# One added to keys and queries by a product of ones in PSUM, and elu+1 as the greater of z+1 and a clipped exponential

## The reference

```python
def _phi(x):
    return jax.nn.elu(x) + 1.0
...
x_norm = _rmsnorm(x, norm_weight)
k = _phi(jnp.einsum('btd,fd->btf', x_norm, Wk))
v = jnp.einsum('btd,ed->bte', x_norm, Wv)
...
def step(M, kv):
    k_t, v_t = kv
    v_pred = jnp.einsum('bf,bfd->bd', k_t, M)
    surprise = jnp.linalg.norm(v_t - v_pred, axis=-1, keepdims=True)
    delta = k_t[:, :, None] * v_t[:, None, :]
    M = M + eta_c[None, :, None] * surprise[:, :, None] * delta
    return (_ln2(M), None)
...
q = _phi(jnp.einsum('btd,fd->btf', x_norm, Wq))
mem_out = jnp.einsum('btf,bfd->btd', q, M)
```

## Time and profile before

| what | value |
|---|---|
| times of three runs | 258.69, 259.81 (median), 259.9 us |
| span of the profiled execution, first to last instruction | 258.2 us |
| what lies around that span, from the times shown | 0.5 to 1.7 us |
| PE busy | 245.4 us, 95% of the span |
| DVE, ACT, POOL busy | 206.3, 186.8, 112.7 us |
| share of PE in the chain that ended last | 66% |
| stretch in which keys and queries are formed | about 13 to 39 us |

### The profile page before, as it was taken

How to read it: one execution, slowest core, us unless ns; L and a number is a source line. 1 busy time by engine, 2 the same in 40 slices (tenths; PEclk the granted TensorE clock), 3 DMA queues, 4 the chain that set the end, 5 groups by cost and what they waited for, 6 DMA issues and landing times.

```text
span 258.2 us, 5143 instructions
## 1 busy us (share of the span) xinstructions
PE 245.4 (95%) x1665; PEld 160.8 (62%) x1665; DVE 206.3 (80%) x694; ACT 186.8 (72%) x459; POOL 112.7 (44%) x148
## 2 busy tenths in 40 slices
PE   7798799999999999999999999999999999999993
PEld 2257554567674458688777767976975444444482
DVE  5998789999968898998899896897623897666684
ACT  1588499986637797887757899989923997777730
POOL 9698300000001689988655795987880000000000
PEclk9999799999999999999999999999999999999999
DMA  7720000000004704000000000000000000000004
GB/s 198 198 57 3 0 1 3 1 0 3 1 1 175 316 3 164 3 0 1 4 0 3 0 0 0 5 0 3 0 0 3 0 0 0 3 3 0 0 30 139
DMA packets 8303, 8.50 MB, mean 33 GB/s; under 512 B 1745, under 2 KB 7378, under 8 KB 7762
## 3 DMA queue, kind: packets, MB, share of 16 engines
q1 hardware_dynamic: 7442, 7.65, 9.1%
q10 hardware_dynamic: 832, 0.49, 0.7%
HBM read 7.09 MB, written 1.05 MB: 32 GB/s over the span
## 4 chain that ended last, share of the span: by engine, by line
PE 66%; DVE 16%; POOL 8%; ACT 4%; issue 3%; DMA 2%; DVEq 0%; SPq 0%; POOLq 0%; ACTq 0%
PE PS L930 11%; PE PS L929 11%; PE PS L902 8%; PE PS L879 7%; PE PS L892 4%; POOL arena L1461 4%; POOL arena L1462 3%; PE PS L693 3%; PE PS L646 3%; PE PS L701 2%; DMA x<-L_attn_x 2%; DVE mxb L1981 2%; DVE arena L1967 2%; PE PS L530 2%; PE PS L685 1%
## 5 line engine op out<-in xcount | busy, mean ns | idle before, releaser
L929 PE MATMUL PS<-arena 128*128 128x512 f16 x128 | 48.5, 379 | 0.0
L930 PE MATMUL PS<-arena 128*128 128x512 f16 x128 | 48.5, 379 | 0.0
L2039 DVE TENSOR_TENSOR arena<-arena 128x512 f32<-128x512 f32 x32 | 22.2, 693 | 13.0 <-ACT arena L1385 13.0
L879 PE MATMUL PS<-arena 128*128 128x512 f32 (+3 forms) x80 | 31.9, 530 | 0.3 <-ACT arena L1354 0.3
L1384 ACT ACTIVATE arena<-PS,arena 128x512 f32<-128x512 f32 x32 | 22.9, 716 | 9.1 <-PE PS L930 9.1
L1461 POOL TENSOR_TENSOR arena<-arena 128x256 f32<-128x256 f32 x32 | 21.6, 674 | 15.4 <-DVE arena L1973 12.9
L1354 ACT ACTIVATE arena<-PS,lnt 128x512 f32<-128x512 f32 (+3 forms) x40 | 24.8, 628 | 2.9 <-DVE lnt L1988 2.8
L1462 POOL TENSOR_TENSOR arena<-arena,small 128x256 f16<-128x256 f32 (+1 forms) x36 | 23.8, 662 | 2.8
L1469 POOL CAST arena<-arena 128x512 f16<-128x512 f32 x2 | 1.3, 636 | 54.3 <-ACT x L1247 54.3
L1385 ACT ACTIVATE arena<-PS,arena 128x512 f16<-128x512 f32 x32 | 22.8, 713 | 0.0
L1981 DVE TENSOR_REDUCE mxb<-PS 128x1 f32<-128x512 f32 (+3 forms) x40 | 22.1, 601 | 0.0
(11 more groups left out here) (291 smaller groups left out, 615.5 us busy)
## 6 DMA issues: line engine op xcount, KB each, us to landing
arena<-h_T SPq DMA_DIRECT2D x2, 1024.0 KB, 6.3
x<-L_attn_x SPq DMA_DIRECT2D x4, 256.0 KB, 4.7
arena<-cos SPq DMA_DIRECT2D x1, 1024.0 KB, 4.8
arena<-sin SPq DMA_DIRECT2D x1, 1024.0 KB, 7.8
arena<-w_T SPq DMA_DIRECT2D x3, 256.0 KB, 3.3
out<-arena SPq DMA_DIRECT2D x2, 256.0 KB, 2.2
con<-shape_constants ACTq DMA_DIRECT2D x1, 192.5 KB, 3.5
out<-arena SPq DMA_DIRECT2D x1, 192.0 KB, 2.0
```

The costliest lines, as they stand in the source:

```text
L879: i = mm(PS[:, k, 0:cnt * P], qT1[:, t * P:(t + 1) * P], kT1[:, c * P:(c + cnt) * P], start=True, stop=not last)
L929: mm(bank(b), wH[:, k, m * P:(m + 1) * P], sH[:, k, cols], start=(k == 0), stop=False)
L930: i = mm(bank(b), wL[:, k, m * P:(m + 1) * P], sL[:, k, cols], start=False, stop=(k == HT4 - 1))
L2039: v.tensor_tensor(RP[m], FP[m], high, ALU.subtract).then_inc(rest_ready, 1)
```

## The change

A third kind of product enters PSUM behind each key and each query product. `one_more` multiplies one row of ones (64 columns as weights) with one row of 512 ones and accumulates it onto the 64 partitions that were just written, so that PSUM holds z+1. ACT then forms exp((z+1) - 1), with the -1 as a bias read from a new constant tile `minus_one`, straight from PSUM, and DVE takes max(min(exp, 1), z+1). The two instructions for a group of keys on ACT become one, and the three for a group of queries become two. The constant is one more memset on POOL; `SET` goes from 16 to 17, and `STATICS` from 8 to 4, since four of ACT's instructions that counted are gone. The copy of z+1 for the second group of queries stays where its max(z, 0) was, behind the four rows.

```diff
             def keys(g):
...
-                    i = mm(PS[F * h:F * h + F, 4 + g, :], wkT[:, :], xrT[:, ch * BANK:(ch + 1) * BANK], start=True, stop=True)
+                    mm(PS[F * h:F * h + F, 4 + g, :], wkT[:, :], xrT[:, ch * BANK:(ch + 1) * BANK], start=True, stop=False)
+                    i = one_more(PS[F * h:F * h + F, 4 + g, :])
                 i.then_inc(k_done, 1)
...
+            def one_more(z):
+
+                return mm(z, warm[0:1, 0:F], warm[0:1, :], start=False, stop=True)
...
-                    i = mm(PS[64 * hf:64 * hf + F, 4 + b, :], wqT[:, :], xrT[:, ch * BANK:(ch + 1) * BANK], start=True, stop=True)
+                    mm(PS[64 * hf:64 * hf + F, 4 + b, :], wqT[:, :], xrT[:, ch * BANK:(ch + 1) * BANK], start=True, stop=False)
+                    i = one_more(PS[64 * hf:64 * hf + F, 4 + b, :])
                 i.then_inc(q_done, 1)
...
-                o.need(o.did(f(e, bank(4 + g), ACT.Relu, scale=-1.0)))
-                f(e, e, ACT.Exp, scale=-1.0).then_inc(kphi_act, 1)
+                f(e, bank(4 + g), ACT.Exp, bias=minus_one).then_inc(kphi_act, 1)
...
+            def queries(b, linear):
+
+                act.wait_ge(q_done, b + 1)
                 cols = slice(b * BANK, (b + 1) * BANK)
-                if negative:
-                    return o.did(f(QE[:, cols], bank(4 + b), ACT.Relu, scale=-1.0))
-                f(QT[:, cols], bank(4 + b), ACT.Relu).then_inc(qphi_act, 1)
+                if linear:
+                    f(QT[:, cols], bank(4 + b), ACT.Copy).then_inc(qphi_act, 1)
+                else:
+                    f(QE[:, cols], bank(4 + b), ACT.Exp, bias=minus_one).then_inc(qphi_act, 1)
...
+            queries(0, False)
+            queries(1, False)
+            queries(0, True)
             table(0)
...
-            relus(1, False)
+            queries(1, True)
...
+            nc.gpsimd.memset(minus_one, -1.0).then_inc(set_once, 1)
...
-                v.scalar_tensor_tensor(out=KU[:, g, 0, 0:BANK], in0=bank(4 + g), scalar=0.0, in1=KE[:, c0 * HALF:c1 * HALF],
-                                       op0=ALU.max, op1=ALU.add).then_inc(k_ready, 1)
+                v.scalar_tensor_tensor(out=KU[:, g, 0, 0:BANK], in0=KE[:, c0 * HALF:c1 * HALF], scalar=1.0, in1=bank(4 + g),
+                                       op0=ALU.min, op1=ALU.max).then_inc(k_ready, 1)
...
-                    v.tensor_tensor(QT[:, part], QT[:, part], QE[:, part], ALU.add).then_inc(q_ready, 1)
+                    v.scalar_tensor_tensor(out=QT[:, part], in0=QE[:, part], scalar=1.0, in1=QT[:, part], op0=ALU.min, op1=ALU.max).then_inc(q_ready, 1)
```

More of the change, by code:

```diff
@@ L56 @@
 EO_EARLY = {9: (0, 1)}
-SET = 16
+SET = 17
 HIGH_TILES = 8
@@ L268, in program @@
         low_scale = small[:, 36:37]
-        eps2 = small[:, 37:38]
+        eps2, minus_one = small[:, 37:38], small[:, 15:16]
         mxs, nbs, rsum, rinv = (lnt[:, i, :] for i in range(2, 6))
@@ L476, in own_squares @@
             return CC[:, 2, 1:HALF + 1, :].rearrange("p j t -> p (j t)")[:, 0:(n - 1) * (L + 1) + 1:L + 1]
-        STATICS = 8
+        STATICS = 4
         def general_path(engine, run):
@@ L1106, in _ @@
                 f(CC[:, 2, r0:r0 + cnt, :], have[:, :, 2 * WINDOW:2 * WINDOW + L], ACT.Copy).then_inc(lanes_act, 1)
-            def relus(b, negative):
+            def queries(b, linear):
+                act.wait_ge(q_done, b + 1)
                 cols = slice(b * BANK, (b + 1) * BANK)
-                if negative:
-                    return o.did(f(QE[:, cols], bank(4 + b), ACT.Relu, scale=-1.0))
-                f(QT[:, cols], bank(4 + b), ACT.Relu).then_inc(qphi_act, 1)
+                if linear:
+                    f(QT[:, cols], bank(4 + b), ACT.Copy).then_inc(qphi_act, 1)
+                else:
+                    f(QE[:, cols], bank(4 + b), ACT.Exp, bias=minus_one).then_inc(qphi_act, 1)
             def table(k):
```

## The result

The changed kernel takes 266.28 us (median of 6 runs, 263.87 to 267.45), the kernel before 259.86 (6 runs, 258.69 to 261.38). The kernel is slower, and its median lies 0.5 us above the forecast. The profiled run took 265.5 us.

What follows compares the result with a forecast made beforehand. TensorE was taken to bound the kernel, with 66% of the chain. 1.25 + 1.75 - 0.55 + 3.65 - 0.15 = 5.95 us more gave 265.8 us, 2.3% slower, range 262.4 to 267.8.

Steps and rivals of the forecast that it cites:

- the pair is split: Keys and queries on PE: lower and upper half, side by side before, start about 1.4 us apart, ones between them.
- Halves together: Rival on PE: upper half overtakes the waiting ones; a group costs 0.37 us more, 260.4 us in all; chance 0.11.
- In order but no drain: Rival on PE: lower half's ones run beside the upper half; a group costs 1.08 us more, 262.7 us; chance 0.13.
- Ones free: Rival: ones cost nothing on PE and the pair stays whole; 0.7 us gained, 259.1 us; chance 0.03.
- What was put at nothing: POOL's memset of -1 (0.1 us without idle cover), DVE's sixteen query sums and L1586, and the counts: no cost.
- A change of footprint: PE, between a half and a product of ones: each change costs 0.15 us, bounds 0.10 and 0.30.
- a group: Each group of keys or queries on PE: 2.66 us instead of 0.91, so 1.75 us more.
- Keys, g = 0: First keys on PE: 1.75 us more, transposes behind swallow 0.5, so PE goes on 1.25 us late.
- Keys, g = 1: Second keys: products end 3.0 us late, one ACT pass fewer saves 0.55, DVE's sum is 2.45 late.
- Queries: Queries on PE start 2.45 us late and cost 3.65 more, so the tables are 6.10 late.
- Scan and all behind it: From ACT's first table copy on, through the scan, everything moves by 5.95 us.
- one stretch at half clock: PE at 1.2 GHz behind its pause: one such stretch kept; none or a second shifts the time by up to 1.75 us.

Runs made afterwards that it cites:

- e2: Changed kernel's order, ones between the halves, but each product of ones reads 128 rows with weights of 1/128 instead of one row; 260.15 us, ratio 0.999.
- e1: Changed kernel with its products reordered: in each group of keys and queries both halves first, then both products of ones; 260.35 us, ratio 0.999.
- e6: Changed kernel, but keys' ones put into PSUM before the inputs arrive, and queries given their one by ACT; 258.58 us, ratio 0.995 to the kernel before.
- e8: Kernel before, without the change, plus five unused products in PE's pause ahead of the lanes' transposes; 258.85 us, ratio 0.995.
- e10: Changed kernel with both halves first, then both products of ones, and PE's pause filled with five unused products; 258.75 us, ratio 0.995.
- e4: Change made to the keys alone, queries as in the kernel before; 261.17 us, ratio 1.005.

## Why the prediction was right

**What held.** The tested mechanism is the forecast's: the pair is split (1.33 us apart, about 1.4 forecast), and a footprint change is the cause, as e2 shows. *Halves together* did not happen, but its price came out for e1, which puts the halves together by its order: 260.4 forecast, 260.35 measured. In e2 a product does pass a waiting one, with the footprint the same. *In order but no drain* (262.7) is out by the group of 2.66 us. *Ones free* is what e6 makes of it: 259.1 forecast, 259.14 in the middle column (258.58 over all, since half its runs are in the first). What was put at nothing cost nothing: the memset took 0.10 us ahead of POOL's idle time, and the sixteen query sums had a median of 217 ns in both kernels.

**Term by term**, from the profiled runs, each with one stretch at half clock. *A change of footprint*: 0.15 was taken; a second pass that held the next for 0.43 without a change holds it 0.52 (13.34 to 13.86), a product of ones 0.33 for 0.22, so 0.10. The second pass of the lower half is this line of the changed kernel, from the view of 13.6 to 13.8 us:

```profile
13.34 0.59 PE L542 MATMUL PS<-arena,wkT 128*64 128x512 f32 x1
```

The further 0.05 is paid by the first pass of a half, not at the ones; a group therefore costs 1.65 more, not 1.75. *Keys, g = 0*: transposes close up by 0.47, 0.5 forecast; PE's next products (L549) start 1.14 late, 1.25 forecast. *Keys, g = 1*: DVE's sum is 2.22 late, 2.45 forecast, with 0.58 for the ACT pass and 0.55 forecast; the bias tile costs what the earlier trace rows said (0.69). *Queries*: they start 2.08 late, 2.45 forecast; the tables 5.70, 6.10 forecast. *Scan and all behind it*: 5.60, 5.95 forecast. The sum is 0.35 too high: 0.23 at the keys and 0.14 between DVE's sum and the queries; what is left cancels. The 0.14 is the lanes' transposes, 2.46 us in the chain in place of 2.62, since the clock fell 0.54 us after their start and not 0.37. The queries' own part came out, 3.62 for 3.65, by luck, with two deviations in it that cancel: 0.20 less for the two groups, and 0.16 more for the half clock, which cost the queries 0.60 before (2.46 in the earlier trace rows, 1.86 in e8) and 0.76 now (1.76 for the first half in the chain, 1.00 for the others). This 0.16 is what the transposes gave up. The span is 5.5 longer, 6.0 forecast.

**What it missed.** The forecast kept one stretch at half clock for both kernels. For the profiled runs that is so, and 265.5 is 0.3 below 265.8. But three of six runs of the changed kernel are in the last column, and this puts the median at 266.28. The small miss of the median is thus two errors of opposite sign, and in part luck: by columns the change costs 5.15 to 5.94, each below the 5.95 of the forecast.

It also took PE as what sets the end behind the lanes' transposes. That is so with the half-clock stretch. Without it, in e8, the chain goes through DVE there:

```profile
30.11 1.60 DVE arena L1636 x3
...
35.03 1.44 DVE arena L1674 x11
```

PE's queries and tables then have time to spare. Queries and tables of e8, and the tables of e10:

```profile
29.69 1.94 PE L615 MATMUL PS<-arena,wqT 128*64 128x512 f32 x8
31.55 2.90 PE L625 MATMUL PS<-arena,con 128*128 128x448 f32 x7
...
31.94 3.27 PE L633 MATMUL PS<-arena,con 128*128 128x448 f32 x8
```

In e10 the tables start 0.39 later at no cost in time, and the chain of e10 goes through PE's queries and tables again, so the spare time is used up. This fits that e1 loses nothing in the first column, 0.49 in the second and 0.63 in the third, and that the changed kernel's loss grows from 5.15 to 5.54; for the last column e1's profile is the only one.

## What to carry to other kernels

A small product that adds a constant is not priced by its own length: ask what runs side by side around it, and whether it lies on the same rows and columns of the array. Put it behind the pair, give it the pair's footprint, or put it into PSUM ahead, while TensorE has nothing to do; the last, with TensorE's pause filled, is the fastest version here (258.03 us, 0.7% faster than the kernel before, and 0.3% faster than the kernel before with its pause filled too). And before a difference of a per cent is read, sort the runs by their granted clock.

## What was not expected of the hardware

In the profiled run of the kernel before, the clock fell to 0.50 behind a pause of PE of 1.40 us, and by their mean clock 61 of 74 runs have such a stretch. Five products of 0.22 us each that nobody reads take this away, worth 1.1 us of the median. The pause is not the whole condition: e6 and e4 have one of 1.42 and 1.41 us at the same place, and their profiled runs kept a clock of 1.00 behind it; by the mean clock half the runs of e6 and seven in ten of e4 have no such stretch. In e6:

```profile
27.41 1.59 PE L610 MATMUL PS<-con,arena 96*128 96x96 f32 x17 [1.42 <-DVE arena L1609]
```

In some runs the stretch is longer. The profiled run of e1 had it over 6.8 us:

```profile
27.80:34.60 6.80, 6.72 (x27) 3.41 (x27) 5.00 (x19) 2.70 (x9) 0.51 (x3) 0.50 0.00 0
```

Its mean clock is 0.986, that of the last column; the middle column's profiles (before, changed) have 3.4 us of it. What decides between none, the short and the long stretch in a run of one kernel was not found.

Two products of float32 over 128 rows and 64 columns, on columns of their own, run side by side pass by pass (four passes in 1.08 us in e1 and e2), two products of one row likewise (0.40 us for both in e1), and one may start before a product that is ahead of it in the program, as e2 shows.
